# Stage 2 of a graph network block: node rows turned by 32x32 blocks on VectorE and a DRAM table, in place of TensorE's transposes

## What is computed

```python
h = relu(layernorm(x))
msg = relu(h[src] + edge_attr)
agg = zeros_like(h).at[dst].add(msg)
t = h + agg
t = t @ W1 + b1                       # 256 -> 512
t = (t - mean) / sqrt(var + eps) * bn_gamma + bn_beta   # over all nodes
y = relu(t) @ W2 + b2                 # 512 -> 256
...                                   # norms over all nodes, relu
x1 = x + h + (the result)
h1 = relu(layernorm(x1))
out = x1 + relu(h1 @ W + segment_sum((h1 @ M)[src], dst))
```

## Time and profile before

| | us |
|---|---|
| median of 3 runs | 2451.24 |
| span of the profiled execution | 2446.4 |
| turn of group 13 to turn of group 97 (first to last TensorE transpose after 600 us) | 604.1 to 1596.1 |
| one group in the steady part of stage 2 | 11.8 |

### The profile page before, as it was taken

One profiled execution on the slowest core, in us unless ns is written; L12 is line 12 of the kernel. 1 busy time (PEld: TensorE's weight loads), 2 busy tenths in 40 slices (PEclk: granted clock), 3 DMA queues, 4 the chain that ended last, 5 costly groups with the idle time before them and its releaser, 6 DMA issues. The chain is left out here.

```text
span 2446.4 us, 48745 instructions
## 1 busy us (share of the span) xinstructions
PE 2354.5 (96%) x12271; PEld 2013.5 (82%) x12271; DVE 2052.5 (84%) x5707; ACT 1713.3 (70%) x3449; POOL 1708.5 (70%) x1599
## 2 busy tenths in 40 slices
PE   7999998799999999999999999979999999989997
PEld 6888886588888888888888888858989888969996
DVE  8999997598888888888888888967777777749996
ACT  6999997466666666666666666638888888846664
POOL 5777777577767667767766666717777777767774
PEclk8999999899999999999999999999999999999999
DMA  8888995323444444444444344349999999765662
GB/s 257 283 278 275 278 277 170 124 58 127 152 150 158 163 151 147 146 146 166 153 147 145 145 164 154 141 173 405 405 411 413 413 413 413 294 197 162 173 177 88
DMA packets 242978, 531.73 MB, mean 217 GB/s; under 512 B 53856, under 2 KB 141177, under 8 KB 231442
## 3 DMA queue, kind: packets, MB, share of 16 engines
q1 hardware_dynamic: 182434, 459.36, 51.2%
q0 software_dynamic: 59808, 70.24, 10.2%
q10 hardware_dynamic: 592, 0.54, 0.1%
HBM read 340.23 MB, written 286.84 MB: 256 GB/s over the span
## 5 line engine op out<-in xcount | busy, mean ns | idle before, releaser
L1020 POOL DMA_INDIRECT ar<-sum_table,idx x392 | 462.3, 1179 | 177.6 <-issue 96.5
L1067 ACT ACTIVATE r<-pair,bnC,bnA 128x512 f32<-128x512 f32 x392 | 305.9, 781 | 380.2 <-PE pair L1268 377.7
L1471 POOL DMA_INDIRECT x1d_table<-x1r,slot x392 | 383.8, 979 | 139.8 <-issue 123.9
L1175 DVE CAST rH<-r 128x512 fp32r<-128x512 f32 x392 | 391.0, 997 | 97.7 <-ACT r L1067 97.7
L1694 PE MATMUL pair<-Ws,h1T 128*128 128x256 f32 x1568 | 358.7, 382 | 8.9 <-DVE orr L1602 7.4
L1694 PEld LDWEIGHTS pair<-Ws,h1T 128*128 128x128 f32 x1568 | 290.2, 190 | 52.1 <-issue 14.3
L1284 PE MATMUL bank<-rH,W2h 128*128 128x512 f32 (+1 forms) x784 | 305.6, 390 | 1.8 <-ACT yr L1081 1.8
L1284 PE MATMUL bank<-rL,W2h 128*128 128x512 f32 (+1 forms) x784 | 305.7, 390 | 0.0
L1284 PE MATMUL bank<-rH,W2l 128*128 128x512 f32 (+1 forms) x784 | 305.0, 389 | 0.0
L836 PE MATMUL bank<-hr 128*128 128x257 f32 (+1 forms) x1568 | 274.2, 329 | 9.6 <-ACT hr L535 9.6
L1184 DVE TENSOR_TENSOR rL<-r,rH 128x512 fp32r<-128x512 f32 x392 | 271.1, 691 | 13.5
(11 more groups left out here) (239 smaller groups left out, 5234.1 us busy)
## 6 DMA issues: line engine op xcount, KB each, us to landing
xr<-in_x SPq DMA_DIRECT2D x186, 512.0 KB, 3.9
xy_kept<-xy_table SPq DMA_DIRECT2D x57, 1024.0 KB, 20.7
x_table<-x1r SPq DMA_DIRECT2D x97, 512.0 KB, 19.8
out<-orr SPq DMA_DIRECT2D x97, 512.0 KB
xy_table<-xr SPq DMA_DIRECT2D x89, 512.0 KB, 2.6
xy_table<-yr SPq DMA_DIRECT2D x89, 512.0 KB, 3.3
xyr<-xy_table SPq DMA_DIRECT2D x32, 1024.0 KB, 21.0
sum_table<-e_tot SPq DMA_DIRECT2D x99, 128.0 KB, 4.5
```

The costliest lines, as they stand in the source:

```text
L1020: pool.indirect_dma_start(ar[0:p, s, j, :], None, sum_table[:, :], bass.IndirectOffsetOnAxis(ap=idx[0:p, s, j:j + 1], axis=0), bounds_chec ...
L1067: act.activation(r32[:, m, 0:n], z_ps[m][:, 0:n], ACT.Relu, bias=bnC[:, m:m + 1], scale=bnA[:, m:m + 1]).then_inc(r_kept, 1)
L1175: dve.tensor_copy(rH[:, s, m, 0:n], r32[:, m, 0:n]).then_inc(rh_kept, 1)
L1471: pool.indirect_dma_start(x1d_table[:, :], bass.IndirectOffsetOnAxis(ap=slot[0:p, part, s * T + j:s * T + j + 1], axis=0), x1r[0:p, s, j, ...
```

## The change

The rows of groups 1 to 96 are no longer turned by TensorE. VectorE transposes each 32 x 32 block of the group's 128 x 1024 tile into a tile `blocks` (the space of W2s), SP stores it to a DRAM table in four DMAs of one quarter of the partitions each (pieces of 512 bytes), and loads the table back in one DMA with the quarters exchanged (`staged`, two slots: the space of Ws and Ms, and that of W1s). ScalarE and VectorE then read the turned rows from SBUF instead of PSUM, through a view in pieces of 32 elements. TensorE still turns groups 0 and 97. All of stage 2 is written out, without loops. Ws and Ms are loaded by SP at the start of stage 3, and TensorE waits for them there. GpSimd's wait before the memset is now on `blocks_made`.

```diff
+    ht_table = nc.dram_tensor("ht_table", (2, QUADS, SQ, KC, QUADS, P), FP32, kind="Internal").ap()
...
-                act.dma_start(Ws[:], W.rearrange("(k p) n -> p k n", p=P)).then_inc(loaded, 16)
-                act.dma_start(Ms[:], M.rearrange("(k p) n -> p k n", p=P)).then_inc(loaded, 16)
...
-        NPEEL = KEPT // NU + 2
+        NPEEL = NG
...
+            return is_int(k) and k in (0, NG - 1)
...
+        blocks = W2s[:].rearrange("p a b -> p (a b)")
+        staged = [WM[:].rearrange("p a b c -> p (a b c)"), W1s[:].rearrange("p a b -> p (a b)")]
...
+                return staged[s][:, c * GC:(c + 1) * GC].rearrange("p (q t n) -> p t q n", q=QUADS, t=T)
...
+                def store_blocks(at):
...
+                    sp.wait_ge(blocks_made, k)
+                    after(sp, ht_in[s], 16 * (turned_before(at) - 1))
+                    for q in range(QUADS):
+                        sp.dma_start(ht_table[s, :, :, :, q, :].rearrange("b p c n -> p c b n"),
+                                     blocks[q * SQ:(q + 1) * SQ, :].rearrange("p (c b n) -> p c b n", c=KC, b=QUADS)
+                                     ).then_inc(ht_out[s], 16)
...
+                def load_turned(at):
...
+                    sp.wait_ge(ht_out[s], 16 * QUADS * turned_before(at))
+                    after(sp, tl_kept, k - 1)
+                    sp.dma_start(staged[s], ht_table[s].rearrange("b p c q n -> (b p) (c q n)")).then_inc(ht_in[s], 16)
...
                     three = back(at, 3)
+                    store_blocks(three)
                     if inside(three, NG) and not stays(three[0]):
...
                         sp.wait_ge(xh2_done, k + 1)
                         sp.dma_start(xh_part(group_block(xy_table, k))[0:p, 0:n, :], xr[0:p, s, 0:n, :]).then_inc(xh_out[s], 16)
+                    load_turned(three)
...
-                        after(pool, t2_made, k - AU + 1)
+                        if is_int(k) and k == AU:
+                            pool.wait_ge(t2_made, 1)
+                        else:
+                            after(pool, blocks_made, k - AU)
...
-                    act.wait_ge(t2_made, k + 1)
+                    if by_tensor(k):
+                        act.wait_ge(t2_made, 1 if k == 0 else 2)
+                    else:
+                        act.wait_ge(ht_in[s], 16 * turned_before(at))
...
-                    keep_high(back(at, -1))
                     pieces = norm(back(at, -2))
                     for m in range(HC):
                         hidden(at, m)
                         for piece in (pieces[0:2], pieces[2:4], [], [])[m]:
                             piece()
+                        if m == 1:
+                            keep_high(back(at, -1))
...
+                def turn_blocks(at):
...
+                    dve.wait_ge(h2_done, k + 1)
+                    after(dve, ht_out[other], 16 * QUADS * turned_before(back(at, 1)))
+                    dve.transpose(blocks.rearrange("p (b t n) -> p t b n", b=KC * QUADS, t=T),
+                                  ar[:, s, :, :].rearrange("p t (b n) -> p t b n", n=SQ)).then_inc(blocks_made, 1)
...
                     stats(back(at, 2), 0)
-                    keep_low(back(at, -1))
                     stats(back(at, 2), 1)
                     high(at, 0)
                     low(at, 0)
                     high(at, 1)
                     low(at, 1)
                     add(back(at, -2))
+                    keep_low(back(at, -1))
+                    turn_blocks(back(at, -2))
...
-                    if not inside(at, NG):
+                    if not inside(at, NG) or not by_tensor(at[0]):
...
+                sp.dma_start(Ws, W.rearrange("(k p) n -> p k n", p=P)).then_inc(w_loaded, 16)
+                sp.dma_start(Ms, M.rearrange("(k p) n -> p k n", p=P)).then_inc(w_loaded, 16)
...
+                        if is_int(k) and k == 0:
+                            pe.wait_ge(w_loaded, 32)
```

More of the change, by code:

```diff
@@ L30 @@
 CA = CH + 16
+SQ = 32
+QUADS = P // SQ
 def back(at, lag):
@@ L190, in gnn_kernel @@
         W2l = sb("W2l", [P, HC, CH], FP32R, scope=weights, side="right")
-        Ws = sb("Ws", [P, KC, CH])
-        Ms = sb("Ms", [P, KC, CH])
+        WM = sb("WM", [P, 2, KC, CH])
+        Ws, Ms = WM[:, 0, :, :], WM[:, 1, :, :]
         vec = sb("vec", [P, 24])
@@ L225, in gnn_kernel @@
         CW = ST * P // SC
-        loaded = sem("loaded")
         consts = sem("consts")
@@ L508, in _ @@
                     edge(t)
-                pool.wait_ge(loaded, 16 * 2)
                 for s in range(EU):
@@ L893, in turn_over @@
             for _ in range(times):
-                pe.matmul(target, ident[:], Ws[:].rearrange("p a b -> p (a b)"), start=True, stop=True)
+                pe.matmul(target, ident[:], W1s[:, 0, :], start=True, stop=True)
         next_phase()
@@ L916, in stays, with by_tensor, turned_before @@
             return is_int(k) and k < KEPT
+        def by_tensor(k):
+            return is_int(k) and k in (0, NG - 1)
+        def turned_before(at):
+            s, used = ring(at, 2)
+            return used + s
+        blocks = W2s[:].rearrange("p a b -> p (a b)")
+        staged = [WM[:].rearrange("p a b c -> p (a b c)"), W1s[:].rearrange("p a b -> p (a b)")]
         x2_in = [sem(f"x2_in{s}") for s in range(NU)]
@@ L927, in gnn_kernel @@
         h2_done = sem("h2_done")
+        blocks_made = sem("blocks_made")
+        ht_out = [sem(f"ht_out{s}") for s in range(2)]
+        ht_in = [sem(f"ht_in{s}") for s in range(2)]
         t2_made = sem("t2_made")
@@ L961, in ybuf, with turned_part, nodes_of @@
                 return y_part(xy_kept[:, k, :, :]) if stays(k) else yr[:, s, :, :]
+            def turned_part(k, s, c, n):
+                if by_tensor(k):
+                    return hT_ps[:, c, 0:n]
+                return staged[s][:, c * GC:(c + 1) * GC].rearrange("p (q t n) -> p t q n", q=QUADS, t=T)
+            def nodes_of(part, k):
+                return part if by_tensor(k) else part.rearrange("p (t q n) -> p t q n", q=QUADS, t=T)
             @block.sync
             def _(sp):
+                def store_blocks(at):
+                    if not inside(at, NG) or by_tensor(at[0]):
+                        return
+                    k = at[0]
+                    s, _ = ring(at, 2)
+                    sp.wait_ge(blocks_made, k)
[5 more added lines that the diff above has]
+                def load_turned(at):
+                    if not inside(at, NG) or by_tensor(at[0]):
+                        return
+                    k = at[0]
+                    s, _ = ring(at, 2)
+                    if is_int(k) and k == 1:
+                        sp.wait_ge(q_made, 1)
+                    sp.wait_ge(ht_out[s], 16 * QUADS * turned_before(at))
+                    after(sp, tl_kept, k - 1)
+                    sp.dma_start(staged[s], ht_table[s].rearrange("b p c q n -> (b p) (c q n)")).then_inc(ht_in[s], 16)
                 def step(at):
@@ L1090, in keep_high @@
                     n = columns(k)
-                    act.wait_ge(t2_made, k + 1)
+                    if by_tensor(k):
+                        act.wait_ge(t2_made, 1 if k == 0 else 2)
+                    else:
+                        act.wait_ge(ht_in[s], 16 * turned_before(at))
                     after(act, z_made, (k - 1) * HC)
                     for c in range(KC):
-                        last = act.activation(tH[:, s, c, 0:n], hT_ps[:, c, 0:n], ACT.Copy)
+                        last = act.activation(nodes_of(tH[:, s, c, 0:n], k), turned_part(k, s, c, n), ACT.Copy)
                     last.then_inc(th_kept, 1)
@@ L1142, in keep_low @@
                     for c in range(KC):
-                        last = dve.tensor_tensor(tL[:, s, c, 0:n], hT_ps[:, c, 0:n],
-                                                 tH[:, s, c, 0:n].bitcast(FP32), ALU.subtract)
+                        last = dve.tensor_tensor(nodes_of(tL[:, s, c, 0:n], k), turned_part(k, s, c, n),
+                                                 nodes_of(tH[:, s, c, 0:n].bitcast(FP32), k), ALU.subtract)
                     last.then_inc(tl_kept, 1)
+                def turn_blocks(at):
+                    if not inside(at, NG) or by_tensor(at[0]):
+                        return
+                    k = at[0]
+                    s, _ = ring(at, AU)
+                    other, _ = ring(back(at, 1), 2)
+                    dve.wait_ge(h2_done, k + 1)
+                    after(dve, ht_out[other], 16 * QUADS * turned_before(back(at, 1)))
+                    dve.transpose(blocks.rearrange("p (b t n) -> p t b n", b=KC * QUADS, t=T),
+                                  ar[:, s, :, :].rearrange("p t (b n) -> p t b n", n=SQ)).then_inc(blocks_made, 1)
                 def stats(at, c):
@@ L1236, in _ @@
                 add((1, 1, 0, NU))
+                turn_blocks((1, 1, 0, NU))
                 keep_low((0, 0, 0, NU))
@@ L1248, in turn @@
                     pe.wait_ge(h2_done, k + 1)
```

(4 more changed lines are left out.)

## The result

The changed kernel takes **3068.81 us** (median of 4 runs, 3065.41 to 3072.76) against 2451.23 us before: a ratio of **1.252**, 95% interval 1.250 to 1.254. Slower by 618 us, where 626 were forecast. The profiled execution has a span of 3063.7 us.

What follows compares the result with a forecast made beforehand. TensorE was taken to bound the kernel before, at 11.8 us per group. With 89 laps of 18.8 us (+623) and seven short laps (+3), the span of 2446.4 became 3072, plus 4.8 for the median 3077 us; range 2970 to 3230.

Steps and rivals of the forecast that it cites:

- the lap through GpSimd and SP's order: Stage 2, one group per lap: turn, memset, gathers, add, store, load, copies, subtractions; 18.8 us; chance 0.87.
- handovers: Term of the stage 2 lap: four handovers between engines at some 0.1 us each, 0.4 us.
- The lap and its count: Stage 2, groups 8 to 96: 89 laps of 18.8 us instead of 11.8, adding 623 us.
- The block transpose: VectorE's turn of a group's blocks, not in the trace: 1.2 us, ends 0.8 and 2.4.
- The short ring: Groups 1 to 7, where SP waits for no add: laps of 12.3 us, adding 3 us in all.
- Reading from SBUF at the same price: ScalarE and VectorE in stage 2: turned rows read from SBUF cost about the same as from PSUM.
- TensorE's clock: Stage 2: part of each group runs at 1.2 GHz, up to 14 us of work instead of 10.9, costing nothing.
- The clock: Rival: TensorE stays at 1.2 GHz in stage 2, 21.8 us of products per group, about 3340 us; chance 0.06.
- The short ring alone: Rival: the add doesn't hold SP, so 96 groups take 12.3 us each, about 2500 us; chance 0.05.
- Faster: Rival: transfers covered, engines bound stage 2, VectorE next at 11.4 us a group, about 2413 us; chance 0.02.
- The side parts: Written-out loops and Ws and Ms loaded in stage 3: hidden by spare DMA time, 0 us in sum.
- The signs named: Changed profile: TensorE 60 to 75% busy, idle 5 to 8 us per group, load 0.4 us after GpSimd's add.

Runs made afterwards that it cites:

- experiment 1: Changed kernel with SP's load of the turned rows moved ahead of its store of x + h: 2602.60 us, ratio 1.062 to the kernel before.
- experiment 2: Changed kernel with GpSimd's add of group k - 2 moved ahead of the memset and gathers of group k: 2593.41 us, ratio 1.058 to the kernel before.
- experiment 3: Changed kernel with GpSimd clearing each slot of ar twice, the second time after a wait: 3224.09 us, ratio 1.316 to the kernel before.
- experiment 9: Kernel before with only stage 2 written out, Ws and Ms loaded in stage 3, and warm-up matmuls reading W1s: 2451.94 us, ratio 1.001.
- experiment 5: Changed kernel with SP's load ahead of the x + h store and VectorE's turn ahead of the subtraction: 2564.24 us, ratio 1.047 to the kernel before.
- experiment 6: On top of experiment 5, GpSimd's add moved ahead of the memset, waiting for VectorE's add of the same group: 2484.68 us, ratio 1.014.
- experiment 7: Changed kernel with load ahead of store, GpSimd's add ahead of memset, row norm three groups ahead in ScalarE's last slots, VectorE reordered: 2482.11 us, ratio 1.014.
- experiment 8: On top of experiment 7, SP stores blocks ahead of the load of x, and the norm returns to ScalarE's first two slots: 2405.56 us, ratio 0.982.

## Why the prediction was right

The cause was the forecast's: the lap through GpSimd and SP's order. Experiments 1, 2 and 3 open it at two places and lengthen it at a third. By the steps of the forecast, the lap from 1205.47 to 1224.19:

| term of the lap | forecast | measured |
|---|---|---|
| memset to the end of the add | 10.1 | 9.62 |
| add to SP's store | 0.1 | 0.02 |
| to the load's issue | 0.4 | 0.73 (0.42 in the next lap) |
| load, to ScalarE's copy | 4.2 | 4.60 |
| copies | 1.1 | 1.18 to VectorE's start |
| subtractions | 1.3 | 1.21 to the turn's start |
| block transpose | 1.2 | 1.24 |
| handovers | 0.4 | 0.12 for the last; the others lie in the terms above |
| sum | 18.8 | 18.72 |

- **The lap and its count** held: 18.76 on average over 88 laps, one fewer than counted (8 to 96 are 89 groups, with 88 distances between them); 88 x (18.76 - 11.8) = 612 of the 616.8 us by which the turn of group 97 is later (2212.9 instead of 1596.1). That the sum is within 0.1 is luck: GpSimd's part was 0.5 too high (the last gather takes 1.0 and not 2.0, as in the short step of the earlier trace rows) and the handovers 0.3, SP's issue of this lap was 0.3 and the load 0.4 too low.
- **The block transpose**, unseen before, took 1.24 us, as the add of the same size. The 2.5 us estimated from the Trainium skill (VectorE: DVE Perf Modes, "The three transpose paths") are not borne out: that lap would have been 20.1. The page's figure is for one 128x128 tile in bf16; here one instruction turned eight such tiles in float32 in half of eight times that figure.
- **The short ring** was mis-sized, 12.3 forecast and (549.2 - 457.3) / 7 = 13.1 measured, some 6 us over seven laps. The laps are 13.9, 12.3, 14.5, 12.6, 13.1, 13.2 and 12.5 us. Two steps failed. From the first block store to the load are 4.4 to 5.4 us, 4.8 on average, where 4.3 were forecast: a quarter takes SP 0.61 us to issue and not 0.43. And VectorE's own work was put at nothing: in the third and the sixth lap its add lay beside GpSimd's, took 3.9 us instead of 1.2, and held the subtraction 2.2 and 1.3 us after ScalarE's copies were done. The third:

```profile
492.86 3.87 DVE L1188 TENSOR_TENSOR ar<-ar,hr 128x1024 f32<-128x1024 f32 x1
496.65 1.28 DVE L1199 TENSOR_TENSOR tL<-W1s,tH 128x512 fp32r<-128x512 f32 x2
```

  The first lap is the start of the stage; ScalarE's copies there did not wait for the load. In the second lap, which no such add held, the steps are 1.3 (turn), 4.8 (stores, to the load), 3.7 (load), 1.2 and 1.3, together the 12.3 of the forecast: the load and the handovers made up for the stores.
- **Reading from SBUF at the same price** held: the subtraction takes 0.69 us instead of 0.68, ScalarE's copy 0.62 instead of 0.61.
- **TensorE's clock** behaved as expected: 0.85 over the stretch, 1.22 us pairs at a group's start, the products of a group done in 12.7 us (1204.25 to 1216.95) of the 18.7, so at no cost, inside the "up to 14 us" of the forecast.
- **The rivals.** The clock: excluded by experiment 3. The short ring alone: this is experiment 1, and even it took 2603 us, not the 2500 that I gave it: from the first block store to the load are 5.4 us there, not 4.3, and from ScalarE's copy to the next turn 2.9, not 2.4. These landings come with more traffic (211 GB/s from 1000 to 1500 us, 151 in the changed kernel); that this is why they are later is not shown. Faster: with the rings opened and SP's queue sorted it is there (2406), near the 2413 worked out for it (11.3 us a group, against 11.4). The nearness is luck: VectorE was to set that pace, and TensorE does, busy 98.9% against VectorE's 95%. And it needed more than an earlier load: the orders of VectorE, GpSimd, ScalarE and SP were all changed.
- **The side parts at nothing**: experiment 9, at most 0.2%.
- **The signs named**: TensorE busy 71.7% and idle 5 to 6 us at each joint; the load 0.4 to 0.7 us behind the store; stage 2 about 1800 us long. The wait of ScalarE for the load came out at 8.4 us in a lap, more than the "4 us and more" written.

## What to carry to other kernels

Before a step is moved to other engines, write down for one group who waits for whom in program order, queues included, and look for a path from the new operation of group j to that of group j + 1: if it closes within one group, its length is the pace, whatever the busy shares say, and no buffer helps. An in-order queue makes neighbours out of strangers: here a load stood behind a store that waited for GpSimd, and later a store behind a load that waited for a landing; moving one line gave 466 us, and moving another, together with the norm's place, 77. A wait that costs nothing today (355 us of it on SP) is the place to look first when something urgent is put behind it.

## What the runs showed of the hardware that was not expected

- VectorE is held up by GpSimd's add more than I had counted. Beside GpSimd's add of 128x1024 (2.4 us), a cast took 3.28 us instead of 0.41, rL 3.30 instead of 0.69, and VectorE's own add 3.87 instead of 1.22 (all in the changed kernel or in experiment 5). Beside the block transpose (experiments 6 to 8) and the statistics (7 and 8) the add ran without delaying either (1.25 and 1.24 us).
- The block transpose of 128x1024 float32 with an output scattered in pieces of 32 elements costs no more than a dense add (1.23 to 1.25 us over 96 instructions).
- Storing a quarter of a tile in pieces of 512 bytes takes SP 0.61 us to issue (median of 384 in the changed kernel), a whole tile in rows of 4 KB 0.33.
